# A rank-64 spectral product on TensorE: two tiles of 64 rows for the building product, groups in pairs, columns of x side by side

## What is computed

```python
o1 = jnp.einsum('jxk,ky,bcxy->jbcxy', cc, dc, xf)
return jnp.einsum('oi,icj,jbcxy->boxy', ac, bc, o1)
...
out1 = _contract_tt(x_ft[:, :, :MODES1, :MODES2], a1, b1, c1, d1)
out2 = _contract_tt(x_ft[:, :, -MODES1:, :MODES2], a2, b2, c2, d2)
```

## Time and profile before

| | |
|---|---|
| median of three runs | 5974.37 us |
| the profiled execution | 5977.58 us, span 5975.8 us |
| TensorE matmul busy | 5432.6 us (91%) |
| TensorE weight load busy | 4915.4 us (82%) |
| VectorE busy | 4316.1 us (72%) |
| ScalarE busy | 3483.7 us (58%) |
| GpSimd busy | 2377.4 us (40%) |
| mean granted clock | 0.954 of 2.4 GHz |

### The profile page before, as it was taken

The page is one execution under the profiler, slowest core; times in us unless marked ns, Lnnn a source line. Parts: engine busy times, 40 slices in busy tenths (PEclk is TensorE's granted clock), DMA queues, the critical chain, the costliest instruction groups (busy, mean ns, idle before and its releaser), DMA issues. The chain is left out here.

```text
span 5975.8 us, 192820 instructions
## 1 busy us (share of the span) xinstructions
PE 5432.6 (91%) x75424; PEld 4915.4 (82%) x75424; DVE 4316.1 (72%) x6707; ACT 3483.7 (58%) x6349; POOL 2377.4 (40%) x2566
## 2 busy tenths in 40 slices
PE   8989989899899898998974999999999999996888
PEld 6778778777777777777764999999999999996888
DVE  7868878788687787887866777777777777762323
ACT  6757757577476675765732666666666666652222
POOL 6747747477475574764720222222222222210000
PEclk9999999999899999999986999999999999998989
DMA  1131121311212213113141222121212121219999
GB/s 51 55 89 55 58 87 51 93 48 56 89 55 69 76 48 97 48 55 90 55 145 57 63 64 64 62 66 60 69 58 69 57 70 56 70 50 348 348 347 317
DMA packets 587637, 562.23 MB, mean 94 GB/s; under 512 B 15092, under 2 KB 540276, under 8 KB 574196
## 3 DMA queue, kind: packets, MB, share of 16 engines
q1 hardware_dynamic: 587124, 554.87, 28.6%
HBM read 286.38 MB, written 268.44 MB: 93 GB/s over the span
## 5 line engine op out<-in xcount | busy, mean ns | idle before, releaser
L1177 DVE TENSOR_TENSOR Ml<-ring,Mh 128x1024 f16<-128x1024 f32 x1024 | 1230.2, 1222 | 546.8 <-ACT Mh L1144 546.7
L1144 ACT ACTIVATE Mh<-ring 128x1024 f16<-128x1024 f32 x1024 | 1027.7, 1023 | 420.2 <-PE ring L1080 412.2
L243 POOL TENSOR_TENSOR Y<-Yf,Y 128x532 f16<-128x532 f32 x1024 | 1210.7, 1196 | 133.0 <-ACT Y L477 90.7
L1079 PE MATMUL ring<-wcur,b_hi 128*128 128x128 f16 x8192 | 1006.8, 219 | 85.0 <-POOL wcur L1034 74.5
L1080 PE MATMUL ring<-wcur,b_lo 128*128 128x128 f16 x8192 | 1005.7, 219 | 0.0
L1079 PEld LDWEIGHTS ring<-wcur,b_hi 128*128 128x128 f16 x8192 | 800.2, 99 | 113.1 <-POOL wcur L1034 74.6
L277 PE MATMUL ring<-uth,A 128*128 128x266 f16 x6144 | 821.7, 284 | 34.9 <-issue 18.5
L1080 PEld LDWEIGHTS ring<-wcur,b_lo 128*128 128x128 f16 x8192 | 802.0, 98 | 29.7
L1091 PE MATMUL ring<-xs,Mh 128*128 128x32 f16 x8192 | 783.3, 219 | 1.0 <-DVE Ml L1177 1.0
L1093 PE MATMUL ring<-xs,Ml 128*128 128x16 f16 x8192 | 778.3, 208 | 0.6 <-issue 0.6
L277 PEld LDWEIGHTS ring<-uth,A 128*128 128x128 f16 x6144 | 614.6, 100 | 195.6 <-issue 31.2
(11 more groups left out here) (138 smaller groups left out, 9592.4 us busy)
## 6 DMA issues: line engine op xcount, KB each, us to landing
xb<-in_x SPq DMA_DIRECT2D x128, 512.0 KB, 4.4
x<-x1b SPq DMA_DIRECT2D x64, 1024.0 KB, 6.3
spec<-sp_out SPq DMA_DIRECT2D x256, 256.0 KB, 2.6
xin<-spec SPq DMA_DIRECT2D x128, 512.0 KB, 6.4
fd<-ft SPq DMA_DIRECT2D x128, 512.0 KB, 4.0
F<-fd SPq DMA_DIRECT2D x8, 8192.0 KB, 27.6
xq<-x SPq DMA_DIRECT2D x128, 512.0 KB, 5.3
out<-xq SPq DMA_DIRECT2D x64, 1024.0 KB, 8.2
```

What stands on the lines that cost most here:

```text
L243: pool.tensor_tensor(Y[:, e, 1, m], Yf[:, m], Y[:, e, 0, m], ALU.subtract).then_inc(e_yl, 1)
L1079: pe.matmul(o, b_hi[:, z, 8 * u + k, :], wcur[:, z, 0, :], start=True, stop=False)
L1144: act.activation(hi, ps, ACT.Copy).then_inc(e_hi, 1)
L1177: dve.tensor_tensor(lo, ps, hi, ALU.subtract).then_inc(e_lo, 1)
```

## The change

- Building: each unit computes each product for two ranks at once, one from rows 0 to 63 and one from rows 64 to 127, into the two banks of its pair. The halves of the rows now hold different ranks (0 to 31 and 32 to 63), w's high and low parts are whole copies in both halves, and hi x hi, hi x lo and lo x hi are three matmuls. A unit has 24 matmuls of 64 rows and 128 columns instead of 16 of 128 rows.
- The 12 groups stand in pairs behind six of the 16 units, not singly behind twelve.
- `xs` has the 32 columns of one y side by side.
- GpSimd's copies of w have no waits between them and no memset before the first; `w_lo` is new.
- `factors` takes the magnitudes from b as it lies for the product and doesn't load it a second time.
- The evacuation writes two runs of 8 ranks for each y instead of one of 16.

```diff
-APP1_AT, OUT_AT, APP0_AT = (2, 3, 4, 5), (7, 8, 9, 10), (11, 12, 14, 15)
+APP1_AT, OUT_AT, APP0_AT = (3, 3, 5, 5), (7, 7, 9, 9), (11, 11, 14, 14)
...
             for z in range(2):
-                sp.dma_start(stage[:, z].rearrange("p i c -> p (i c)"), bn_d[z],
-                             max_dma_last_dim=4096).then_inc(s_ld[z], 16)
-            for n, (z, c) in enumerate(chunks):
-                e = n % 2
-                if n < 2:
-                    sp.wait_ge(f_bm[e], 1)
-                else:
-                    sp.wait_ge(f_lo[e], n // 2)
-                sp.dma_start(stage[:, e], bst_d[z, :, CH * c:CH * c + CH]).then_inc(s_ld[e], 16)
+                sp.dma_start(stage[:, z], bst_d[z]).then_inc(s_ld[z], 16)
...
-            dve.tensor_copy(w_st[:, :, :, 0, :], wf[:]).then_inc(f_w, 1)
+            dve.tensor_copy(w_hi[:, :, :, 0, :], wf[:]).then_inc(f_w, 1)
             dve.wait_ge(f_w, 1)
+            dve.tensor_tensor(w_lo[:, :, :, 0, :], wf[:], w_hi[:, :, :, 0, :], ALU.subtract).then_inc(f_w, 1)
+            dve.wait_ge(f_w, 2)
+            for w in (w_hi, w_lo):
+                for t in (0, 64):
+                    dve.tensor_scalar(w[t:t + 32, :, :, 1, :], w[t + 32:t + 64, :, :, 0, :], -1.0, None, ALU.mult)
+                    dve.tensor_copy(w[t + 32:t + 64, :, :, 1, :], w[t:t + 32, :, :, 0, :])
             for z in range(2):
...
+                dve.wait_ge(f_hi, z + 1)
+                dve.scalar_tensor_tensor(out=b_lo[:, z], in0=stage[:, z], scalar=inv[:, 0:1], in1=b_hi[:, z],
+                                         op0=ALU.mult, op1=ALU.subtract)
...
-        xs = sb("xs", [128, 2, 2, 2, B, MODES], F16)
+        xs = sb("xs", [128, 2, MODES, 2, 2, B], F16)
...
-                for k in range(8):
-                    o = ring[:, UNIT_PAIR[n], k // 4, 128 * (k % 4):128 * (k % 4) + 128]
-                    pe.matmul(o, b_hi[:, z, 8 * u + k, :], wcur[:, z, 0, :], start=True, stop=False)
-                    mm = pe.matmul(o, b_lo[:, 8 * u + k, :], wcur[:, z, 1, :], start=False, stop=True)
-                mm.then_inc(p_bld, 1)
+                for k in range(4):
+                    for part, (b, w) in enumerate(((b_hi, 0), (b_hi, 1), (b_lo, 0))):
+                        for t in range(2):
+                            r = slice(64 * t, 64 * t + 64)
+                            mm = pe.matmul(ring[:, UNIT_PAIR[n], t, 128 * k:128 * k + 128], b[r, z, 4 * u + k, :],
+                                           wcur[r, z, w, :], start=(part == 0), stop=(part == 2))
+                            if k == 3 and part == 2:
+                                mm.then_inc(p_bld, 1)
...
-                    pe.matmul(o, Mh[:, z, y, :], xs[:, z, :, :, :, y].rearrange("p v r b -> p (v r b)"),
+                    pe.matmul(o, Mh[:, z, y, :], xs[:, z, y].rearrange("p v r b -> p (v r b)"),
...
-            return (ring[:, UNIT_PAIR[8 * z + u]].rearrange("c k (m y) -> c y (k m)", y=MODES),
-                    Mh[:, z, :, 16 * u:16 * u + 16],
-                    Ml[:, z, :, 16 * u:16 * u + 16])
+            return (ring[:, UNIT_PAIR[8 * z + u]].rearrange("c k (m y) -> c y k m", y=MODES),
+                    Mh[:, z].rearrange("c y (k m) -> c y k m", k=2)[:, :, :, 8 * u:8 * u + 8],
+                    Ml[:, z].rearrange("c y (k m) -> c y k m", k=2)[:, :, :, 8 * u:8 * u + 8])
```

More of the change, by code:

```diff
@@ L785, in _, with phase2 @@
             steps(dve, first, body, last, drain)
-def phase2(nc, spec, bn_d, bst_d, cst_d, dst_d, am_d, alt_d, fd):
+def phase2(nc, spec, bst_d, cst_d, dst_d, am_d, alt_d, fd):
     with ExitStack() as ctx:
@@ L791, in sb, with factors @@
             return ctx.enter_context(nc.sbuf_tensor(name, shape, dt))
-        b_hi = sb("b_hi", [128, 2, RANK_I, C], F16)
-        b_lo = sb("b_lo", [128, RANK_I, C], F16)
-        w_st = sb("w_st", [128, 2, MODES, 2, MODES], F16)
+        b_hi = sb("b_hi", [128, 2, RANK_I // 2, C], F16)
+        b_lo = sb("b_lo", [128, 2, RANK_I // 2, C], F16)
+        w_hi = sb("w_hi", [128, 2, MODES, 2, MODES], F16)
+        w_lo = sb("w_lo", [128, 2, MODES, 2, MODES], F16)
         am = sb("am", [128, 2, 2, 2 * C])
[L797 to L805, removed]
+        factors(nc, bst_d, cst_d, dst_d, am_d, alt_d, b_hi, b_lo, w_hi, w_lo, am)
+        modes(nc, spec, b_hi, b_lo, w_hi, w_lo, am, fd)
+def factors(nc, bst_d, cst_d, dst_d, am_d, alt_d, b_hi, b_lo, w_hi, w_lo, am):
     with ExitStack() as ctx:
@@ L817, in factors @@
         wf = sb("wf", [128, 2, MODES, MODES])
-        stage = sb("stage", [128, 2, CH, C])
+        stage = sb("stage", [128, 2, RANK_I // 2, C])
         ext = sb("ext", [128, 6])
@@ L837, in factors @@
         f_hi = sem("f_hi")
-        f_lo = [sem("f_lo0"), sem("f_lo1")]
         consts = ((cst, cst_d), (dst, dst_d), (am, am_d), (alt, alt_d))
-        chunks = [(z, c) for z in range(2) for c in range(RANK_I // CH)]
         block = ctx.enter_context(nc.Block())
@@ L879, in _ @@
             act.wait_ge(f_sc, 1)
[L880 to L884, removed]
+            for z in range(2):
+                act.activation(b_hi[:, z], stage[:, z], ACT.Copy, scale=inv[:, 0:1]).then_inc(f_hi, 1)
         @block.vector
@@ L930, in _, with modes @@
             dve.wait_ge(k[5], 1)
-            dve.tensor_copy(w_st[:, :, :, 0, :], wf[:]).then_inc(f_w, 1)
+            dve.tensor_copy(w_hi[:, :, :, 0, :], wf[:]).then_inc(f_w, 1)
             dve.wait_ge(f_w, 1)
-            for z in range(2):
[L934 to L949, removed]
+            dve.tensor_tensor(w_lo[:, :, :, 0, :], wf[:], w_hi[:, :, :, 0, :], ALU.subtract).then_inc(f_w, 1)
[4 more added lines that the diff above has]
+                    dve.tensor_copy(w[t + 32:t + 64, :, :, 1, :], w[t:t + 32, :, :, 0, :])
+            for z in range(2):
+                dve.wait_ge(f_hi, z + 1)
+                dve.scalar_tensor_tensor(out=b_lo[:, z], in0=stage[:, z], scalar=inv[:, 0:1], in1=b_hi[:, z],
+                                         op0=ALU.mult, op1=ALU.subtract)
+def modes(nc, spec, b_hi, b_lo, w_hi, w_lo, am, fd):
     with ExitStack() as ctx:
@@ L989, in aux_groups @@
             for first, at, kind in ((0, APP1_AT, "app1"), (4, OUT_AT, "out"), (8, APP0_AT, "app0")):
-                if n in at:
-                    j = at.index(n)
-                    yield first + j, kind, j
+                for j in range(4):
+                    if at[j] == n:
+                        yield first + j, kind, j
         block = ctx.enter_context(nc.Block())
@@ L1024, in _ @@
         def _(pool):
-            pool.memset(wcur[:], 0.0).then_inc(w_zero, 1)
-            pool.wait_ge(w_zero, 1)
             def current(s, z):
[L1029 to L1036, removed]
+                for part, w in ((0, w_hi), (1, w_lo)):
+                    pool.tensor_copy(wcur[:, z, part, :], w[:, z, bass.ds(s, 1)].rearrange("p s v y -> p (s v y)")
+                                     ).then_inc(w_cur[z], 1)
             def convert(s, z):
-                src = xin[:, z].rearrange("p b r y -> p r b y")
+                src = xin[:, z].rearrange("p b r y -> p y r b")
                 pool.wait_ge(x_ld[z], 16 * (s + 1))
@@ L1043, in convert @@
                 carry(pool, carried)
[L1044 removed]
+                pool.tensor_copy(xs[:, z, :, 0], src).then_inc(x_hi[z], 1)
                 pool.wait_ge(x_hi[z], s + 1)
[L1046 removed]
+                pool.tensor_tensor(xs[:, z, :, 1], src, xs[:, z, :, 0], ALU.subtract).then_inc(x_cv[z], 1)
                 pool.wait_ge(x_cv[z], s + 1)
@@ L1053, in _ @@
             with pool.Fori(1, MODES) as s:
-                pool.wait_ge(p_bld, 16 * s - 8)
+                pool.wait_ge(p_bld, 32 * s - 16)
                 carry(pool, carried)
                 current(s, 0)
-                pool.wait_ge(p_bld, 16 * s)
+                pool.wait_ge(p_bld, 32 * s)
                 carry(pool, carried)
@@ L1090, in apply @@
                     o = ring[:, AUX, bank, 32 * n:32 * n + 32]
-                    pe.matmul(o, Mh[:, z, y, :], xs[:, z, :, :, :, y].rearrange("p v r b -> p (v r b)"),
+                    pe.matmul(o, Mh[:, z, y, :], xs[:, z, y].rearrange("p v r b -> p (v r b)"),
                               start=True, stop=False)
-                    mm = pe.matmul(o[:, 0:16], Ml[:, z, y, :], xs[:, z, 0, :, :, y].rearrange("p r b -> p (r b)"),
+                    mm = pe.matmul(o[:, 0:16], Ml[:, z, y, :], xs[:, z, y, 0].rearrange("p r b -> p (r b)"),
                                    start=False, stop=True)
@@ L1141, in build @@
             def build(s, n):
-                act.wait_ge(p_bld, 16 * s + n + 1)
+                act.wait_ge(p_bld, 32 * s + 2 * n + 2)
                 ps, hi, _lo = unit(*divmod(n, 8))
@@ L1355, in _, with program @@
                     dve.tensor_tensor(x_, x_, ring[:, 4 + k % 4, :], ALU.add).then_inc(e_o, 1)
-def program(nc, x, ut, dt, dtail, mask, dfth, dftw, ones, bn, bst, cst, dst, am, alt, iy, ix, out):
```

(5 more changed lines are left out.)

5 lines of the change are left out of this document (1 added, 4 removed).

## The result

The changed kernel takes 5684.49 us (median of four runs, 5676.09 to 5689.48) against 5973.82 us before, a ratio of 0.951 (95% interval 0.9496 to 0.9524). The forecast was 5709 us. Its profiled execution took 5676.09 us, span 5673.9, where the sum had 5712. An execution that shows a lower granted clock and lies over 1.5% above the fastest of its kernel is left out of what is compared here; that concerns two of the four of e5_x_step8 (6150.67 and 6159.27 us) and no other.

The account below looks back on a forecast made before the run. TensorE's issue was taken to bound the middle stage. Saving 4.07 us in each of 63 iterations (256 us) and 10 elsewhere brings the profiled 5977.6 to 5711.6 us, told as 5709 for the median; range 5655 to 5895.

Parts of the forecast that it names:

- account by distances: Middle stage before the change: TensorE work summed from distances between matmul starts, 32.6 us plus two waits, gives 33.1 an iteration.
- Overlap of the tiles: Building product: each pair of 64-row matmuls costs one stream, so a unit takes 0.67 us.
- Rival A: Building product: the tiles do not overlap, a unit takes 1.33 us, 6256 us in all; chance 0.12.
- Change of tiling: TensorE switching between 64-row and 128-row matmuls: 0.17 us for entering and leaving, 1.0 us an iteration for six pairs.
- Applications at 27 ns: Application matmuls with columns of x side by side start 27 ns apart instead of 43.7: 0.87 us a group.
- Rival B: Applications: few columns, not the stride, set 43.7 ns; groups stay at 1.40 us, 5891 us in all; chance 0.08.
- The wait at unit 1: In the run of five units, unit 1 waits for unit 15's banks to be evacuated: 1.87 us late, before 0.25.
- the walk: Stepping through an iteration's units, groups and evacuations in order to find TensorE's waits: 3.0 us in all.
- Setting up: Before the loop: fewer half-height products and waits save 7 us, the memset 0.7; with 2 for the tail, together 10.
- the splitting of x for nothing: GpSimd's strided reading of x stays hidden even three times slower (9.5 us), so it costs nothing.
- Rival D: Evacuation: ScalarE and VectorE pay 10% for shorter runs, +1.8 us an iteration, 5822 us in all; chance 0.04.
- Rival C: Middle stage: the clock falls in the 1.87 us wait, 1.7 us an iteration lost, 5816 us in all; chance 0.10.

Follow-up runs that it names:

- e5_x_step8: The changed kernel with the columns of x 16 bytes apart: 6032.47 and 6056.34 us.
- e4_tiles_in_turn: The changed kernel with all 12 matmuls of one 64-row tile before the other tile's 12, not alternating: 6036.39 us, ratio 1.0099 to the kernel before.
- e1_x_only: The kernel before with only the columns of x put side by side: 5776.40 us, ratio 0.9669.
- e5_x_step2: The changed kernel with the columns of x 4 bytes apart: 5689.03 us, ratio 0.952 to the kernel before.
- e6_spread: The changed kernel with its pairs of groups behind units 2, 5, 8, 11, 13 and 15: 5566.95 us, ratio 0.9319 to the kernel before.
- e8_spread_strided_x: e7_spread_banks with the columns of x 128 bytes apart again: 5926.86 us, ratio 0.9922 to the kernel before.
- e2_tiles_strided_x: The changed kernel with the columns of x 128 bytes apart again: 6037.93 us, ratio 1.011 to the kernel before.
- e3_single_groups: The changed kernel with its 12 groups singly behind 12 units, as before the change: 5731.02 us, ratio 0.9593 to the kernel before.
- e7_spread_banks: e6_spread with the order of the three bank pairs also turned by 11 units: 5539.08 us, ratio 0.9272 to the kernel before.

## Why the prediction was right

**TensorE's issue was the limit, and the account by distances closed.** Right. The same account for the changed kernel: 16 x 0.67 + 8 x 0.80 + 4 x 1.78 + 1.0 for changes of tiling = 25.2 us. Waits of about 3.2 by the distances between starts (2.7 of them idle time in the record) make 28.4 of the measured 28.7.

**Overlap of the tiles: a unit of 0.67 us.** Right: 0.67, six matmuls in 0.17 us. e4_tiles_in_turn shows that alternation is what brings it. Rival A was overpriced all the same: tiles in turn still overlap where they meet, 0.93 us from unit to unit instead of 1.33.

**Change of tiling, 0.17 us for both ways.** Right: 0.15 instead of 0.06 from a unit to an application (4006.07 to 4006.22), and 0.10 instead of 0.025 back to a unit (4007.81 to 4007.91).

**Applications at 27 ns.** Mis-sized, on the cautious side: 25 ns, 0.80 us a group instead of 0.87. That is 0.6 us an iteration, 35 us in all, more than the whole difference between forecast and result; somewhat longer waits took part of it back. An iteration is 28.7 us instead of 29.0, 20 us in all. The profiled execution lies 35.5 us below the sum: these 20, some 2.5 of the setting up and the tail, and the 13.5 us in phase 1 and the last stage, whose code is the same, which are chance. Rival B fell with e1_x_only and e5_x_step2.

**The wait at unit 1.** Right in place and size: the walk had the unit 1.87 us late; between starts the trace has 1.87 us in place of a step of 0.06, so 1.81 late, and 1.65 of them are idle time after the last result. All idle time for VectorE before a unit is 105.1/48.8 = 2.2 us an iteration (walk: 1.9 + 0.5), those before applications 25.6/48.8 = 0.5 (walk: 0.5). e6_spread confirms the cause, a run of five units: without the run this idle time is 26.2 us in 1200 instead of 90.0, and never above 0.4 at a time.

**Setting up, 8 us, and the splitting of x for nothing.** Right: 7.5 us (the prediction's 10 has 2 more for the tail behind the loop); the splitting rose from 3.2 to 4.7 us and TensorE never waited for it. Rival D did not happen: the evacuations took the time they took before.

**The clock.** The forecast was 1.00, and the changed kernel has 1.00. Rival C named the wait at unit 1 as what brings it down. The wait is neither enough nor needed. The changed kernel has it in every iteration; one stretch with it:

```profile
4000.30:4003.70 3.40, 1.64 (x50) 1.35 (x48) 3.17 (x5) 2.43 (x4) 1.38 (x3) 1.00 0.72 263
```

And e8_spread_strided_x, which has none, is at 0.92; there, in e2_tiles_strided_x and in e5_x_step8 the stretch before each fall has no idle time at all. Yet the wait may have a part. In e3_single_groups and e4_tiles_in_turn, kernels with columns side by side, every fall comes behind a stretch with such a wait (TensorE busy 2.4 to 2.6 and 2.07 of 3.41 us). What the kernels with a fall in the profiled execution share is the 64-row tiles, and with them strided applications, groups standing singly, or tiles in turn. No kernel with the 128-row product shows one in the middle stage. Which property of the tiles does it, their half use of the rows or the pauses at a change, was not tried, and the cause stays open. The changed kernel is not far from it: with its groups placed singly the clock falls nine times in 1200 us. The prediction's reason, dense units on both sides of the wait, fits the changed kernel, but no run tests it; that this part came true may be luck.

## What to carry to other kernels

Judge a stream of short matmuls by the distance between their starts, and when it lies above 25 to 30 ns look at how the moving columns lie in memory before anything else: side by side, or at least four to 16 bytes, as in e5_x_step2. A reordering that makes TensorE faster moves the limit to the evacuation, so place the other work so that no run of units is longer than the ring of banks can carry; here that was worth half as much again as the change itself (145 and 289 us). Take the parts of a change apart even when it wins as a whole: here two of them cost time on their own. Read the granted clock of the stage in each of these runs, for a part can look bad by the clock alone.

## What the runs showed of the hardware that was not expected

- Two 64-row tiles in alternation start 3 matmuls each in 0.17 us, the pace of one 128-row stream. The Trainium skill, "TensorEngine Tiling (Array Packing)", Key Properties, says that different tiles can run loads and matmuls in parallel, which this agrees with, and that a change of mode drains the engine; that costs 0.09 us on the way from the tiles to 128 rows and 0.08 us back.
- Two such tiles one after the other, 12 matmuls each, still overlap by three matmuls where they meet: 0.93 us from unit to unit in e4_tiles_in_turn, not 24 x 56 ns.
- Matmuls of 128 rows and 16 or 32 columns, four or more columns to 16 bytes, start 25 ns apart (4 bytes from column to column or contiguous); with columns 16 or 128 bytes apart, about 44.
- TensorE's granted clock can fall with no idle time in the record: 0.92 in e8_spread_strided_x, with TensorE busy 1200.00 of 1200 us, against 1.00 in e7_spread_banks with 1180.86. An iteration is 1.9 us longer there than the walk for a full clock has it. And it can hold with much idle time: 1.00 in the changed kernel, with TensorE busy 1082.81 us of 1200.
